# A graph layer's output product made with nodes on the PSUM partitions, the residual put in by identity products

## The chip, the core and the metric

One core of one Trainium2 chip runs the whole kernel. The metric is the device time of one execution in microseconds (us); for the kernel before it is the median of three runs. A measurement of this kernel can tell a difference of about 0.5% (3.3 us) from none.

## What is computed

Two graph layers over N = 3125 nodes with 128 features and 53125 edges, each with a residual and a layer norm over the features:

```python
x = _layernorm(x + L0(x, src, dst, edge_type_32, edge_weight1, weight, w_comp, bias))     # called x1 below
x = _layernorm(x + L1(x, edge_attr_128, src, dst, eps, W1, b1, gamma, beta, W2, b2))

def L1(node_feat, edge_feat, src, dst, eps, W1, b1, gamma, beta, W2, b2):
    msg = node_feat[src] + edge_feat
    neigh = jax.ops.segment_sum(msg, dst, num_segments=node_feat.shape[0])
    h = ((1.0 + eps[0]) * node_feat + neigh) @ W1 + b1           # N x 256
    h = (h - mean(h, axis=0)) * rsqrt(var(h, axis=0) + 1e-05) * gamma + beta
    return jax.nn.relu(h) @ W2 + b2                              # N x 128
```

The batch norm needs the mean and the variance over all nodes of every one of the 256 units, so nothing of the output layer can start before the last node's h is there. What the change touches is all behind that point: relu, the product with W2, the residual with x1, the second layer norm, the stores.

## The kernel before, in words

The first 619 us make L0, x1 and the neighbour sums of L1: a long unrolled loop over edge tiles in `narrow_sums` (TensorE, VectorE and ScalarE each have one), with gathers on GpSimd's queue, then a last series of block products on TensorE (L1041) whose results VectorE adds into the sums (L1439, two adds for a block). The order there is written out: `FINALS` lists the blocks, first those called `FILLS`, then 13 more; each product goes to one of six PSUM banks (`FINAL_BANKS`), and TensorE waits for a bank's add of six blocks ago. A flag chooses between this "narrow" way and a "wide" one for other inputs; the runs here take the narrow one.

Everything is kept **transposed**, features on the 128 partitions and nodes on the free axis: `sums[:, B, :]` holds the input of W1, `x1_t` holds x1, and `hidden` (two planes of 3125 columns, float32) holds h. The nodes are cut in seven chunks: k = 0 to 5 with 512 nodes, which is one PSUM bank of float32, and k = 6 with the 53 left over (`REST`). A chunk has four tiles of 128 nodes.

The last stage, from about 619 us on, has these steps:

- TensorE `into_hidden` (L1176): W1 stationary, 512 nodes moving, two products for a chunk, into banks 0, 1 (even chunks) or 2, 3 (odd). ScalarE `keep_hidden` (L880) adds b1 and copies to `hidden`. VectorE `hidden_stats` (L1609) takes batch-norm statistics.
- The batch norm: VectorE aggregates (L1615), ScalarE takes a square root (L885), VectorE makes scale and shift (L1617 to L1620) and signals `bn_ready`.
- The output layer, a pipeline over the chunks with two slots s = k % 2. ScalarE `relu_hidden` (L891) writes relu(scale h + shift) to `relu_stage`, two instructions for a chunk. TensorE `into_out` (L1188) multiplies it with W2 stationary into bank s, out again transposed. VectorE `second_residual` (L1625) adds b2 and x1 and writes `layer_stage` in SBUF. TensorE `turn_out` (L1139, in `turn_chunk`) transposes it tile by tile into bank 2 + s, now with nodes on the partitions. VectorE `second_stats` takes mean and variance over the features (L1557, L1560, in `statistics`), ScalarE the square root (L861), VectorE `second_shift` reciprocal and shift (L1640, L1642), and ScalarE `normalise_out` (L897) writes the normalised tiles to `out_stage`. SP's queue stores a chunk (L675) when its tiles are there.

`chunk_pipeline` writes the order on each engine: for a step it calls the stages at their lags, in the given order, first two steps unrolled, then a loop over pairs, then the rest. On ScalarE the order of a step is relu of chunk k, normalise of k - 3, square root of k - 2; on VectorE shift of k - 2, statistics of k - 1, residual of k; on TensorE product of k, transposes of k - 1. `relu_hidden` of chunk k waits for `out_mm` of chunk k - 2, since the relu buffers are two. Every engine takes its instructions in order. A float32 product appears in the trace as two weight loads and two matmuls.

`normalise` (L1562) exists for the first layer norm of the wide way; the same arithmetic in the narrow way is `chunk_norm` (L1400): VectorE subtracts the mean and multiplies by the reciprocal deviation, both [P, 1] operands.

## Time and profile before, and how to read it

| what | us |
|---|---|
| median of three runs (lowest, highest) | 666.05 (664.55, 668.14) |
| the profiled execution's own time | 670.06 |
| its span, first to last instruction | 668.2 |
| TensorE busy in the span | 545.4 (82%) |
| VectorE | 488.7 (73%) |
| GpSimd (gathers) | 414.0 (62%) |
| ScalarE | 303.5 (45%) |
| mean granted TensorE clock, share of full | 0.872 |

PE is the matmul side of TensorE and PEld its weight loads; DVE is VectorE, ACT ScalarE, SPq the DMA queue of SyncE. In the views, times are us from the start of the span unless marked ns; "L1188" is line 1188 of the kernel; an instruction's form is partitions x elements of output and input. PEclk is the granted clock as a share of 2.4 GHz, 0.50 being 1.2 GHz. A timeline row is start, duration, engine, line, operation, tiles, shape and count; several instructions that follow each other are one row, and a row's duration runs from the first one's start to the last one's end. A single instruction's own duration is longer than the step to the next one, since they overlap.

### The profile page before, as it was taken

Reading aid. Unit: us, or ns where it says so; the run is one execution under the profiler, and the core shown is the slowest. Engines: PE = TensorE matmul, PEld = TensorE weight load, DVE = VectorE, ACT = ScalarE, POOL = GpSimd, SP = SyncE. Lnnn points to the kernel's source line nnn. Section 1 sums busy time; section 2 is a strip of 40 time slices with the busy share of each in tenths; the row PEclk is TensorE's granted clock in tenths of the full one; section 3 lists DMA queues with packets and bytes.
Section 4 is the critical chain, followed back from the end, with each engine's and each line's share of the span. In section 5 each row is a group of like instructions: output and inputs, shape, how many; then the busy total and the mean of one; then the engine's idle time right before and its main releaser. Section 6 shows DMA issues by size and latency. Waiting matters only on the chain.

```text
span 668.2 us, 13132 instructions
## 1 busy us (share of the span) xinstructions
PE 545.4 (82%) x3874; PEld 439.0 (66%) x3874; DVE 488.7 (73%) x1852; ACT 303.5 (45%) x689; POOL 414.0 (62%) x434
## 2 busy tenths in 40 slices
PE   4779777877798868888797889598986999999774
PEld 3569676567685757766786758586765887767231
DVE  6998988679976678884798856988648883541535
ACT  9736545464442544533544435344434452100656
POOL 6777777777777777777777777777777740000000
PEclk9978769787787869897789879798979899999977
DMA  5424667555756366584566656757747469700003
GB/s 129 117 53 126 190 182 192 170 136 166 222 158 205 112 175 204 163 248 138 171 184 194 213 164 199 216 165 245 236 107 241 123 183 366 281 1 2 0 10 89
DMA packets 96220, 108.21 MB, mean 162 GB/s; under 512 B 10757, under 2 KB 80630, under 8 KB 96146
## 3 DMA queue, kind: packets, MB, share of 16 engines
q1 hardware_dynamic: 80082, 79.25, 38.0%
q0 software_dynamic: 13312, 27.29, 15.2%
q10 hardware_dynamic: 2752, 0.79, 0.6%
q8 instruction: 33, 0.54, 0.4%
q14 instruction: 41, 0.34, 0.2%
HBM read 81.73 MB, written 25.56 MB: 161 GB/s over the span
## 4 chain that ended last, share of the span: by engine, by line
PE 38%; DVE 25%; POOL 13%; issue 9%; DMA 5%; ACT 5%; DVEq 3%; SPq 1%; ACTq 0%
POOL gathered_flat L707 13%; PE psum L1041 12%; PE psum L1016 7%; PE psum L986 7%; DVE etype_hot L1370 5%; PE psum L992 4%; DVE sums_flat L1479 4%; PE psum L1007 4%; DVE etype_hot L1367 3%; DVE weighted L1291 3%; DVE adj_flat L1455 2%; DVE adj_flat L1267 2%; DMA gathered_flat<-in_x_dram,src_i 2%; DMA adjacency<-adj_flat 2%; PE psum L1176 1%
## 5 line engine op out<-in xcount | busy, mean ns | idle before, releaser
L707 POOL DMA_INDIRECT gathered_flat<-in_x_dram,src_i x416 | 411.7, 990 | 129.1 <-issue 123.1
L986 PE MATMUL psum<-weighted,gathered_flat 128*128 128x160 f32 (+1 forms) x832 | 162.7, 326 | 38.4 <-DMA gathered_flat<-in_x_dram,src_i 16.3
L986 PEld LDWEIGHTS psum<-weighted,gathered_flat 128*128 128x128 f32 x832 | 145.6, 224 | 54.8 <-issue 34.6
L794 ACT ACTIVATE gathered_flat<-psum 128x25 f16<-128x25 f32 x182 | 35.0, 192 | 238.2 <-PE psum L1007 231.6
L1370 DVE TENSOR_SCALAR etype_hot<-iota_key,key_t 128x300 f16<-128x300 f16 (+1 forms) x416 | 134.1, 324 | 0.0
L1479 DVE TENSOR_TENSOR sums_flat<-psum,sums_flat 128x180 f32 x208 | 71.6, 344 | 84.3 <-PE psum L992 56.2
L770 ACT ACTIVATE adj_flat<-zero_col 128x450 f16<-128x450 f32 x208 | 107.9, 574 | 42.3 <-DMA adjacency<-adj_flat 31.9
L992 PEld LDWEIGHTS psum<-hot,attrs 128*128 128x128 f32 x832 | 126.2, 217 | 0.0
L992 PE MATMUL psum<-hot,attrs 128*128 128x20 f32 (+1 forms) x832 | 121.7, 263 | 0.0
L1007 PE MATMUL psum<-etype_hot 128*128 128x300 f16 (+2 forms) x624 | 108.7, 286 | 0.0
L796 ACT ACTIVATE adj_flat<-psum 128x475 f32 x182 | 107.3, 590 | 0.2 <-issue 0.2
L1367 DVE TENSOR_SCALAR etype_hot<-iota_key,gathered_flat 128x128 f16<-128x128 f16 x416 | 104.9, 252 | 0.2
L1041 PE MATMUL psum<-sums_flat 128*128 128x288 f16 (+1 forms) x546 | 76.6, 297 | 3.3 <-DVE sums_flat L1439 3.2
L1007 PEld LDWEIGHTS psum<-etype_hot 128*128 128x128 f16 x624 | 68.5, 133 | 8.9
L1291 DVE TENSOR_TENSOR weighted<-hot,coef 128x640 f32<-128x640 f32 x104 | 72.7, 739 | 1.8
L1041 PEld LDWEIGHTS psum<-sums_flat 128*128 128x128 bf16 (+1 forms) x546 | 54.0, 101 | 23.3 <-issue 8.9
L1455 DVE TENSOR_TENSOR adj_flat<-gathered_flat,adj_flat 128x25 f16 x182 | 47.9, 263 | 21.0 <-DVE adj_flat L1455 14.8
L1439 DVE TENSOR_TENSOR sums_flat<-psum,sums_flat 128x144 f32 x124 | 37.7, 304 | 33.3 <-PE psum L1041 17.6
L1016 PE MATMUL psum<-sums_flat,gathered_flat 128*128 128x512 f32 (+1 forms) x112 | 53.7, 617 | 4.3 <-DVE sums_flat L1439 4.3
L1041 PE MATMUL psum<-coef,sums_flat 128*128 128x288 f16 x294 | 45.1, 309 | 9.9 <-DVE sums_flat L1439 9.8
L1041 PEld LDWEIGHTS psum<-coef,sums_flat 128*128 128x128 bf16 x294 | 29.9, 105 | 21.8 <-issue 13.2
L1016 PEld LDWEIGHTS psum<-sums_flat,gathered_flat 128*128 128x128 f32 x112 | 20.6, 211 | 20.2 <-issue 20.1
(143 smaller groups left out, 356.4 us busy)
## 6 DMA issues: line engine op xcount, KB each, us to landing
attrs<-in_edge_attr_dram SPq DMA_DIRECT2D x51, 512.0 KB
adjacency<-adj_flat SPq DMA_DIRECT2D x26, 900.0 KB, 4.9
gathered_flat<-in_x_dram,src_i POOLq DMA_INDIRECT x416
sums_flat<-adjacency SPq DMA_DIRECT2D x11, 576.0 KB, 6.5
coef<-adjacency SPq DMA_DIRECT2D x20, 288.0 KB, 6.7
sums_flat<-adjacency SPq DMA_DIRECT2D x6, 648.0 KB, 7.6
sums_flat<-adjacency SPq DMA_DIRECT2D x10, 288.0 KB, 6.4
etype_hot<-adjacency SPq DMA_DIRECT2D x1, 1656.0 KB, 10.3
```

The lines of the kernel that those rows point to most:

```text
L707: pool.indirect_dma_start(gathered[:, t % (RING * GROUP), :], None, x[:, :], bass.IndirectOffsetOnAxis(src_i[:, t:t + 1], 0)).then_inc(gat ...
L770: piece = nc.scalar.activation(adj_ring[:, s, j * size:(j + 1) * size], zero_col[:, 0:1].to_broadcast([P, size]), ACT.Copy)
L796: nc.scalar.activation(target[:, :, bass.ds(places[u % GU] + 1, WIN - 1)], counts[:, :, 1:WIN], ACT.Copy).then_inc(counts_copied, 1)
L986: nc.tensor.matmul(ps[:, 0:B, STARTS[i]:STARTS[i] + WIDTHS[i]], gathered[:, (u * UNIT + i) % (RING * GROUP), 0:F], weighted_tiles(s, i)[:, ...
L992: last = nc.tensor.matmul(ps[:, B, STARTS[i]:STARTS[i] + WIDTHS[i]], attrs[:, s * GROUP + j, :], hot_tiles(s, i)[:, u % GU, :], start=(i = ...
L1007: last = nc.tensor.matmul(adj_counts(u)[:, :, lo:hi], low_hot[:, u % KEYRING, i, :], source[:, :, lo - STARTS[i]:hi - STARTS[i]], start=(i ...
L1016: product = nc.tensor.matmul(bank, w_base[:, b, :], sums[:, b, k * CHUNK:k * CHUNK + n], start=(b == 0), stop=(b == B - 1))
L1041: product = nc.tensor.matmul(psum[:, bank, 0:BLOCK * SPREAD], x1_part(k, c)[0:rows, i * F:(i + 1) * F], counts[0:rows, :, :], start=(h == ...
L1291: last = nc.vector.tensor_tensor(weighted_tiles(s % 2, i), hot_tiles(s % 2, i).unsqueeze(2).to_broadcast([P, HALF, B, n]), coef[:, g * GRO ...
L1367: nc.vector.tensor_scalar(low_hot[:, u % KEYRING, i, :], iota_key[:, 0:P], low_t[:, t:t + 1], None, ALU.is_equal)
L1370: last = nc.vector.tensor_scalar(key_hot[:, u % KEYRING, i, 0:n], iota_key[:, 0:n], key_t[:, t:t + 1], None, ALU.is_equal)
L1479: nc.vector.tensor_tensor(window, unit_psum(u), window, ALU.add).then_inc(added, 1)
```

## The change

Relu is written in place in `hidden`. The output is made with nodes on the partitions: a relu tile (128 units x 128 nodes) is stationary and W2's half (128 x 128) moves, so a tile's output needs no transpose. Each chunk has a PSUM bank of its own (`OUT_BANKS`, seven of the eight). Before them, x1 with b2 added is put in the same banks by products of x1's tiles (stationary) with the identity (moving), with `start` on a bank's first tile and no `stop`, so that the W2 products accumulate on it; TensorE has these behind `into_hidden` in its queue, with a wait for the banks that `keep_hidden` still reads. b2 is added to x1 beforehand, in place, by one VectorE instruction over 128 x 3125 (`bias_x1`), put behind the third of the last 13 block adds. `second_residual`, `turn_out`, `second_shift` and `normalise_out` are gone; VectorE normalises with `normalise` (reciprocal, then one tensor_scalar for a tile out of PSUM with two [P, 1] operands). Its order is statistics of k, normalise of k - 1. ScalarE's is relu of k, square root of k - 2. The pipeline's loops are unrolled.

```diff
@@ -143,6 +143,8 @@
+    ALL_CHUNKS = tuple((k, CHUNK) for k in range(CHUNKS)) + ((CHUNKS, REST),)
+    OUT_BANKS = (4, 5, 6, 7, 2, 3, 0)
@@ -328,7 +330,6 @@
-        relu_stage = sums[:, 2:4, 0:2 * CHUNK].rearrange("p s (j n) -> p s j n", j=2)
@@ -670,12 +668,13 @@
-            def store_out(k, s, n):
-                wait_alone(sp, out_ready, (k + 2) * CT + len(tiles_of(n)))
-                sp.dma_start(rows_of(out, k, n), out_stage[:, bass.ds(k * CT, CT), :] if n == CHUNK
+            def store_out(k, n):
+                sp.wait_ge(out_ready, k * CT + len(tiles_of(n)))
+                sp.dma_start(rows_of(out, k, n), out_stage[:, k * CT:(k + 1) * CT, :] if n == CHUNK
...
-            chunk_pipeline(sp, store_out)
+            for k, n in ALL_CHUNKS:
+                store_out(k, n)
@@ -885,28 +883,23 @@
-            def relu_hidden(k, s, n):
-                act.wait_ge(out_mm, k + 1)
+            def relu_hidden(k, n):
...
-                    nc.scalar.activation(relu_stage[:, s, j, 0:n], hidden[:, j, span(k, n)], ACT.Relu,
-                                         bias=bn_shift[:, j:j + 1], scale=bn_scale[:, j:j + 1]).then_inc(relu_ready, 1)
-            def normalise_out(k, s, n):
-                act.wait_ge(shift_ready, k + 1)
-                for i, rows in tiles_of(n):
-                    nc.scalar.activation(out_stage[0:rows, bass.ds(k * CT + i, 1), :].rearrange("p t f -> p (t f)"),
-                                         psum[0:rows, 2 + s, i * P:(i + 1) * P], ACT.Identity,
-                                         bias=ln_shift[0:rows, s, i:i + 1],
-                                         scale=ln_rstd[0:rows, s, i:i + 1]).then_inc(out_ready, 1)
-            chunk_pipeline(act, relu_hidden, None, deviations(1), normalise_out, order=(0, 3, 2))
+                    units = hidden[:, j, k * CHUNK:k * CHUNK + n]
+                    nc.scalar.activation(units, units, ACT.Relu, bias=bn_shift[:, j:j + 1],
+                                         scale=bn_scale[:, j:j + 1]).then_inc(relu_ready, 1)
+            for k, n in ALL_CHUNKS:
+                relu_hidden(k, n)
+                if k >= 2:
+                    deviations(1)(k - 2, k % 2, CHUNK)
+            for k, n in LATE_CHUNKS:
+                deviations(1)(k, k % 2, n)
...
-            pe.sem_inc(out_mm, 2)
-            pe.sem_inc(out_turned, 2)
@@ -1179,22 +1172,30 @@
-            pe.wait_ge(bn_ready, 1)
-            def into_out(k, s, n):
-                pe.wait_ge(relu_ready, k * 2 + 2)
-                pe.wait_ge(out_t_ready, k + 1)
+            def x1_into_out(k, n):
+                if OUT_BANKS[k] < 4:
+                    pe.wait_ge(hidden_ready, 18 if OUT_BANKS[k] < 2 else 16)
+                for i, rows in tiles_of(n):
+                    first = k * CHUNK + i * P
+                    nc.tensor.matmul(psum[0:rows, OUT_BANKS[k], i * P:(i + 1) * P], x1_t[:, first:first + rows],
+                                     ident[:, :], start=(i == 0), stop=False)
+            pe.wait_ge(x1_biased, 1)
+            for k, n in ALL_CHUNKS:
+                x1_into_out(k, n)
+            def into_out(k, n):
...
-                    last = nc.tensor.matmul(psum[:, s, 0:n], w2_sb[:, j, :], relu_stage[:, s, j, 0:n],
-                                            start=(j == 0), stop=(j == 1))
+                    pe.wait_ge(relu_ready, 2 * k + j + 1)
+                    for i, rows in tiles_of(n):
+                        first = k * CHUNK + i * P
+                        last = nc.tensor.matmul(psum[0:rows, OUT_BANKS[k], i * P:(i + 1) * P],
+                                                hidden[:, j, first:first + rows], w2_sb[:, j, :],
+                                                start=False, stop=(j == 1 and (i + 1) * P >= n))
...
-            def turn_out(k, s, n):
-                pe.wait_ge(out_t_ready, k + 3)
-                pe.wait_ge(out_ready, k * CT + CT)
-                turn_chunk(2 + s, layer_stage[:, s, :], n).then_inc(out_turned, 1)
-            chunk_pipeline(pe, into_out, turn_out)
+            for k, n in ALL_CHUNKS:
+                into_out(k, n)
@@ -1524,7 +1524,13 @@
+                    if n == len(FILLS) + 2:
+                        bias_x1()
...
+            def bias_x1():
+                nc.vector.tensor_scalar(x1_t[:, :], x1_t[:, :], b2_col[:, 0:1], None, ALU.add).then_inc(x1_biased, 1)
@@ -1601,6 +1607,7 @@
+                bias_x1()
@@ -1619,30 +1626,22 @@
-            def second_residual(k, s, n):
-                dve.wait_ge(out_mm, k + 3)
-                dve.wait_ge(out_turned, k + 1)
-                nc.vector.scalar_tensor_tensor(layer_stage[:, s, 0:n], psum[:, s, 0:n], b2_col[:, 0:1],
-                                               x1_t[:, span(k, n)], ALU.add, ALU.add).then_inc(out_t_ready, 1)
-            def out_tile(s, i, rows):
-                return psum[0:rows, 2 + s, i * P:(i + 1) * P]
-            def second_stats(k, s, n):
-                dve.wait_ge(out_turned, k + 3)
-                statistics(1, k, s, n, lambda i, rows: out_tile(s, i, rows))
-            def second_shift(k, s, n):
-                c, top = len(tiles_of(n)), min(n, P)
-                dve.wait_ge(ln_std_ready[1], k + 1)
-                dve.wait_ge(out_ready, k * CT + CT)
-                nc.vector.reciprocal(ln_rstd[0:top, s, 0:c], ln_std[0:top, s, 0:c]).then_inc(ln_rstd_ready[1], 1)
-                dve.wait_ge(ln_rstd_ready[1], k + 1)
-                nc.vector.scalar_tensor_tensor(ln_shift[0:top, s, 0:c], ln_mv[0:top, s, 0:c, 0], -1.0,
-                                               ln_rstd[0:top, s, 0:c], ALU.mult, ALU.mult).then_inc(shift_ready, 1)
-            chunk_pipeline(dve, second_residual, second_stats, second_shift, order=(2, 1, 0))
+            def out_tile(k, i, rows):
+                return psum[0:rows, OUT_BANKS[k], i * P:(i + 1) * P]
+            def second_stats(k, n):
+                dve.wait_ge(out_mm, k + 1)
+                statistics(1, k, k % 2, n, lambda i, rows: out_tile(k, i, rows))
+            def second_norm(k, n):
+                normalise(1, k, k % 2, n, lambda i, rows: out_tile(k, i, rows),
+                          lambda i, rows: out_stage[0:rows, k * CT + i, :], out_ready)
+            for k, n in ALL_CHUNKS:
+                second_stats(k, n)
+                if k:
+                    second_norm(k - 1, CHUNK)
+            second_norm(CHUNKS, REST)
```

## Rows read from the trace of the kernel before

**Rows 1.** The page, chain that ended last: its share by engine.
```profile
PE 38%; DVE 25%; POOL 13%; issue 9%; DMA 5%; ACT 5%; DVEq 3%; SPq 1%; ACTq 0%
```

**Rows 2.** Busy time, clock and DMA in stretches of the last stage.
```profile
core 0: us, PE busy (x) PEld busy (x) DVE busy (x) ACT busy (x) POOL busy (x), PEclk, DMA share, GB/s
619.00:632.20 13.20, 11.27 (x28) 4.75 (x28) 6.12 (x11) 7.83 (x12) 0.00 (x0) 1.00 0.00 1
632.20:634.20 2.00, 0.00 (x0) 0.00 (x0) 1.57 (x4) 1.98 (x5) 0.00 (x0) 0.98 0.00 0
634.20:636.60 2.40, 0.00 (x0) 0.00 (x0) 1.83 (x9) 0.97 (x3) 0.00 (x0) 0.50 0.00 0
...
638.20:644.20 6.00, 6.00 (x7) 2.44 (x8) 0.75 (x1) 2.81 (x4) 0.00 (x0) 0.50 0.00 0
644.20:665.10 20.90, 12.93 (x47) 5.98 (x45) 13.73 (x70) 15.63 (x40) 0.00 (x0) 0.91 0.23 64
```

**Rows 3.** The chain in order of time, first products to the first statistics.
```profile
638.18 6.75 PE psum L1188 x8
644.93 0.45 PE psum L1139 x4
645.40 0.90 DVE ln_part L1557 x4
```

**Rows 4.** Timeline of VectorE, a chunk in the steady part.
```profile
654.34 0.89 DVE L1557 BATCH_NORM_STATS2 ln_part<-psum 128x6 f32<-128x128 f32 x4 [0.56 <-PE psum L1139]
655.38 0.38 DVE L1560 BATCH_NORM_AGGREGATE ln_mv<-ln_part 128x2 f32<-128x6 f32 x4 [0.15 <-DVE ln_part L1557]
655.78 0.75 DVE L1625 SCALAR_TENSOR_TENSOR attrs<-psum,b_col,sums_flat 128x512 f32<-128x512 f32 x1
656.45 0.17 DVE L1640 RECIPROCAL ln_rstd<-ln_std 128x4 f32<-128x4 f32 x1
...
657.35 0.89 DVE L1557 BATCH_NORM_STATS2 ln_part<-psum 128x6 f32<-128x128 f32 x4 [0.54 <-PE psum L1139]
```

**Rows 5.** Timeline of TensorE and ScalarE around the batch norm.
```profile
624.53 7.60 PE L1176 MATMUL psum<-sums_flat,gathered_flat 128*128 x20 [1.08 <-ACT sums_flat L880]
...
636.57 2.93 ACT L891 ACTIVATE sums_flat<-sums_flat,bn_shift,bn_scale 128x512 f32<-128x512 f32 x4 [0.82 <-DVE bn_shift L1620]
```

**Rows 6.** Timeline, end of the kernel: the last ScalarE tile and the last stores.
```profile
664.36 1.29 SPq L675 DMA_DIRECT2D out_dram<-gathered_flat  x2
...
664.56 0.45 ACT L897 ACTIVATE gathered_flat<-psum,ln_shift,ln_rstd 53x128 f32<-53x128 f32 x1 [0.41 <-DVE ln_shift L1642]
```

**Rows 7.** Timeline of TensorE at full clock, 545 to 562 us.
```profile
556.82 0.65 PE L986 MATMUL psum<-weighted,gathered_flat 128*128 128x160 f32 x4
557.30 0.52 PE L992 MATMUL psum<-hot,attrs 128*128 128x20 f32 x4
```

**Rows 8.** Timeline of TensorE at the low clock, 42 to 54 us.
```profile
48.46 1.19 PE L986 MATMUL psum<-weighted,gathered_flat 128*128 128x160 f32 x4
```

**Rows 9.** VectorE instructions by form, busy us and mean ns of one.
```profile
L1400 DVE TENSOR_SCALAR sums_flat<-sums_flat,ln_mv,ln_rstd 128x128 f32<-128x128 f32 x4 | 1.1, 342 | 0.0
L1410 DVE TENSOR_SCALAR sums_flat<-sums_flat 128x512 bf16<-128x512 f32 x1 | 0.4, 427 | 0.0
L1412 DVE TENSOR_TENSOR sums_flat<-sums_flat 128x512 f32<-128x512 f32 x1 | 0.7, 693 | 0.0
L1383 DVE TENSOR_TENSOR sums_flat<-psum,attrs 128x512 f32<-128x512 f32 x1 | 0.7, 692 | 6.3 <-PE psum L1024 6.3
L1267 DVE TENSOR_SCALAR adj_flat<-psum,relation_col 128x512 bf16<-128x512 f32 x26 | 18.1, 730 | 0.3 <-PE psum L923 0.3
```

**Rows 10.** Timeline of VectorE, normalising a chunk of the first layer norm.
```profile
574.57 1.12 DVE L1400 TENSOR_SCALAR sums_flat<-sums_flat,ln_mv,ln_rstd 128x128 f32<-128x128 f32 x4
```

**Rows 11.** Timeline of VectorE, block adds before the last stage.
```profile
609.46 0.76 DVE L1439 TENSOR_TENSOR sums_flat<-psum,sums_flat 128x144 f32 x2 [1.29 <-PE psum L1041]
...
618.85 0.76 DVE L1439 TENSOR_TENSOR sums_flat<-psum,sums_flat 128x144 f32 x2 [8.64 <-PE psum L1041]
```

More of the change, by code:

```diff
@@ L342, in gnn_resnorm_kernel @@
         ln_rstd = sb("ln_rstd", [P, 2, CT])
-        ln_shift = sb("ln_shift", [P, 2, CT])
         psum = ctx.enter_context(nc.psum_tensor("psum", [P, 8, 512], F32))
@@ L458, in gnn_resnorm_kernel @@
         out_mm = sem("out_mm")
-        out_t_ready = sem("out_t_ready")
-        out_turned = sem("out_turned")
-        shift_ready = sem("shift_ready")
+        x1_biased = sem("x1_biased")
         out_ready = sem("out_ready")
@@ L735, in _ @@
             act.sem_inc(agg_relu, 2)
-            act.sem_inc(out_ready, 2 * CT)
             act.sem_inc(x1_t_ready, 2)
@@ L1214, in _ @@
             dve.sem_inc(res_ready[0], 2)
-            dve.sem_inc(out_t_ready, 2)
             dve.wait_ge(const_ready, 2)
```

## The prediction, made before the changed kernel was run

> **What bounds the kernel now.** I read the page's chain first. It gives 38% of the span to TensorE and 25% to VectorE [rows 1], but that is an average over a long front part that the change leaves alone, so the reader should go on to the stretches of the last stage [rows 2]. Four things are to be seen there. TensorE ends `into_hidden` at 624.53 + 7.60 = 632.1 us [rows 5] and then has nothing to do while VectorE and ScalarE make the batch norm. Its clock falls from full to 0.50 (1.2 GHz) in that idle time, at about 634.2, and is still 0.50 from 638.2 to 644.2 although PE is busy without a gap [rows 2]. In the chain, the first eight output matmuls therefore take 6.75 us, then come the transposes, and VectorE's first statistics start at 645.40 [rows 3], 8.8 us behind the scale and shift (ready at 636.57, when the first relu starts [rows 5]). From then on the work goes by chunks: statistics start at 654.34 and again at 657.35, a period of 3.01 us, in which VectorE waits 0.54 us for transposes [rows 4]. The last tile is normalised at 664.56 + 0.45 = 665.0 and the last store lands at 668.2, a tail of 3.2 us [rows 6].
>
> So there are two places for a gain: the 8.8 us before the first statistics, and the period.
>
> **The start.** The change puts 25 identity products (six chunks of four tiles, one of one) into the batch norm's time. Each is a float32 product of 128 columns, two weight loads and two matmuls. The nearest rows are the products of 160 and 120 columns at full clock: four matmuls with their loads go from 556.82 to 557.30, so 0.12 us for one [rows 7]. The row's 0.65 is three such steps and the last one's own latency, 0.29. With 20 columns the four take 0.52 [rows 7]; less a latency of 0.25, a little shorter, that is 0.09 a step, which is the weight load alone. So at 140 columns the load is mostly hidden behind the matmul before. I take 0.24 us for a product; bounds 0.19 (load alone) and 0.43 (load and matmul one after the other, 2 x (0.09 + 0.12)). 25 x 0.24 = 6.0 us, from 632.1 to 638.1. The relu of chunk 0 is ready at 636.57 + 2 x 0.73 = 638.0 (four relus take 2.93 [rows 5]). So the identity products fit the gap almost exactly; what of them is past 638.0 costs 0.1 us. The banks of chunks 4 to 6 wait for `keep_hidden`, long done when TensorE comes to them.
>
> Chunk 0 then needs 8 W2 products instead of four wide matmuls: 8 x 0.24 = 1.9 us, done at 640.1, statistics at 640.2. Before, 645.4. That is 5.2 us earlier, of which some 3.4 are the clock (6.75 us at half clock for two chunks, 3.4 at full) and the rest the missing residual add and transposes. It rests on the clock staying full, since TensorE no longer idles; rows 2 show it full from 619 to 632 at 85% busy.
>
> **The period.** VectorE loses the residual add (0.75 [rows 4]), the shift and the 0.54 us of waiting. It keeps statistics, 0.89 + 0.15 + 0.38 = 1.42, with its wait 1.47, and gains the normalising: reciprocal 0.17 [rows 4], 0.04 for its semaphore, and four tensor_scalars out of PSUM with two [P, 1] operands. The same instruction from SBUF takes 1.12 us for four, 0.26 from start to start [rows 9, 10]. From PSUM there is one nearby row: 128x512 takes 730 ns against 427 from SBUF, 303 more for 512 elements [rows 9]. Tensor_tensor shows no such difference (692 from PSUM, 693 from SBUF [rows 9]), so it is likely a rate by element and a quarter of it, 0.076, at 128. Bounds 0.26 (none) and 0.56 (all 303 ns at any width); I take 0.30, nearer to the quarter. Normalising a chunk is then 0.21 + 1.20 = 1.41, and VectorE's period 1.47 + 1.41 = 2.88 against 3.01: nearly nothing is gained there.
>
> The Trainium skill ("VectorE: DVE Perf Modes", Why PSUM operands drop a tier) says an SBUF float32 tensor_scalar runs at two elements a cycle and one from PSUM at one. By that rule, the trace agrees: the tensor_scalar from SBUF is faster than the tensor_tensor, the one from PSUM is not. Its table of costs (section on the TRN2 errata) has a larger fixed cost from PSUM besides, 120 cycles for 58; by it a tile would take some 0.13 us more than from SBUF, 0.39, and the end would come 2 us later than I forecast. The equal tensor_tensor rows speak against that.
>
> ScalarE's relus (1.47 a chunk) and square roots stay under 2.88, and TensorE's 1.92 too; each chunk has its own bank, so TensorE waits for relus only. The square root of chunk k - 2 sits ahead of the relu of chunk k + 1 in ScalarE's queue and waits there for the statistics; that relu is then needed one period later, by a TensorE that is ahead. It costs nothing while VectorE is the slowest.
>
> **The sum.** Chunk 1's products end at 640.1 + 1.9, its statistics start at 642.1. From there VectorE has no wait: statistics of 1, 1.47; six normalisations, 8.46; statistics of 2 to 5, 5.88; the short chunk's statistics and normalisation, one tile each, an estimate of 0.6 and 0.55. Together 17.0, so 659.1. Before 665.0: 5.9 us earlier. The tail: the two last stores now follow 0.55 us apart in place of 1.0, and SP's queue needs 1.29 us to issue two [rows 6], so up to 0.4 us is given back; I take 0.3. Net 5.6 us.
>
> **bias_x1.** One instruction of 3125 elements; at 427 ns for 512 it is 2.6 us, at 693 it is 4.2 [rows 9]. It sits between block adds, where VectorE idles 1.29 us before each add and 8.64 before the last, 618.85 [rows 11]. The three or four adds behind it come late and catch up; TensorE waits only for the add of six blocks ago, some 12 us. Cost nothing; without that cover, 2.6 to 4.2. The unrolled loops and the dropped semaphores: nothing that a row shows.
>
> The profiled execution took 670.06 us with a span of 668.2; the change would make that 662.6 and 664.5. It is 4.0 us over the median of 666.05, from which I subtract the same 5.6: **660.4**.
>
> **Rivals.**
>
> - **VectorE dearer** (the normalising binds). At 0.39 a tile the end is 2.2 us later: saving 3.4, 662.6. At the far bound, 0.56, a period of 3.9 us: six times 1.04 more, end 665.3, no gain, 666.6. For it: no row has this instruction from PSUM. Against: the tensor_tensor pair. Chance 0.14, half of it past the 0.5% line.
> - **The clock falls all the same.** If identity products do not keep it up, it falls at 634.2 as before [rows 2]. The 16 products left then take twice as long (the four matmuls of 0.65 us take 1.19 at the low clock [rows 7, 8]), which delays all by some 4 us; the clock returns after some 6 us of work. End 663 to 665, saving 0 to 2: 664 to 666. Chance 0.12.
> - **TensorE becomes the bound, and the kernel slower.** One mechanism: the weight load of every 128 columns is not hidden, or the clock stays low through the stage. A product costs 0.43 to 0.48, the identity products end at 643 to 644, a chunk takes 3.4 to 3.8 us, more than VectorE. End 669 to 672: 4 to 7 us slower, 670 to 673. It decides from 0.37 us for a product: there the gain is nil. For it: 50 more weight loads than needed before, and no row with 128-column moving operands of this kind. Against: the rows of 160 and 120 columns. Chance 0.08.
> - **It doesn't do what it says:** the W2 products start late for another reason, such as ScalarE's queue (a relu behind a square root) or the stores crowding at the end. Saving 1 to 3: 663 to 665. Chance 0.08.
>
> **How the numbers follow.** The forecast has 0.58: 658.5 to 662 with the bounds of a product (0.19 makes it 1.5 earlier) and of a tile (0.26 and 0.335: 1 us either way). The range goes to the first two rivals, 658.3 to 665.0, and leaves out 2 in 10. Faster by over 0.5% (3.3 us; the resolution of a measurement here): 0.58 + 0.07 + a little of the last = 0.67. Slower: 0.08. Same: 0.25.
>
> **What would show it.** The clock in stretches after 632: 1.00 up to 650. TensorE busy without a gap from 632.1, the last identity product near 638. First statistics at 640.2. Four tensor_scalars out of PSUM in 1.3 us or less, VectorE without idle time from the statistics of chunk 1 on. Block adds at the same times from the sixth behind bias_x1 on. The last tile at 659, the tail 3.5. A first statistics start past 644 would make the clock or the product's price wrong; a period over 3.1 the tile's.

## The result, and the profile after

| | before | changed |
|---|---|---|
| median of eight runs each on one chip, us | 667.21 | 661.44 |
| lowest, highest | 664.55, 669.91 | 659.68, 664.44 |
| ratio, with its 95% interval | | 0.9917 (0.989 to 0.9944) |
| profiled execution, its span | 670.06, 668.2 | 664.44, 662.6 |
| mean granted TensorE clock | 0.872 | 0.889 |

The changed kernel is 5.5 us faster at the ratio (667.2 x 0.0083), with an interval of 3.7 to 7.3 us; the spans differ by 5.6. That is past the 0.5% that a measurement here resolves, but not by much. The stretches of the last stage of the changed kernel (columns as in [rows 2]):

```profile
613.80:627.00 13.20, 11.06 (x55) 6.22 (x53) 2.96 (x6) 3.83 (x6) 0.00 (x0) 1.00 0.01 2
...
633.00:639.00 6.00, 6.00 (x53) 5.70 (x53) 2.84 (x11) 4.55 (x9) 0.00 (x0) 1.00 0.00 0
...
639.00:650.00 11.00, 10.64 (x94) 10.13 (x92) 8.76 (x46) 8.22 (x16) 0.00 (x0) 1.00 0.17 49
```

Where [rows 2] had TensorE without work and a clock that fell to 0.50 at 634.2 and stayed there to 644.2, it is now busy for all of 633 to 639 and the clock reads 1.00 up to 650. The timeline from there:

```profile
624.77 7.61 PE L1169 MATMUL psum<-sums_flat,gathered_flat 128*128 x20 [1.07 <-ACT sums_flat L878]
...
632.21 5.94 PE L1180 MATMUL psum<-ident,sums_flat 128*128 128x128 f32 x50
...
636.82 4.34 ACT L889 ACTIVATE sums_flat<-sums_flat,bn_shift,bn_scale 128x512 f32<-128x512 f32 x6 [0.82 <-DVE bn_shift L1627]
...
638.08 11.23 PE L1192 MATMUL psum<-gathered_flat,sums_flat 128*128 128x128 f32 x96
640.17 0.89 DVE L1563 BATCH_NORM_STATS2 ln_part<-psum 128x6 f32<-128x128 f32 x4 [3.39 <-PE psum L1192]
...
641.96 0.89 DVE L1563 BATCH_NORM_STATS2 ln_part<-psum 128x6 f32<-128x128 f32 x4 [0.36 <-PE psum L1192]
```

The fifty matmuls of the identity products (x1 into the banks) follow the last product of W1 and end where the W2 products begin, 638.1. The first layer-norm statistics start at 640.17; in [rows 3] it was 645.40. From the second statistics on, VectorE waits for no other engine. A chunk in the steady part, against [rows 4], and the one place where VectorE stops:

```profile
644.76 0.88 DVE L1563 BATCH_NORM_STATS2 ln_part<-psum 128x6 f32<-128x128 f32 x4
...
645.79 0.38 DVE L1566 BATCH_NORM_AGGREGATE ln_mv<-ln_part 128x2 f32<-128x6 f32 x4
646.09 0.15 DVE L1571 RECIPROCAL ln_rstd<-ln_std 128x4 f32<-128x4 f32 x1
...
646.27 1.37 DVE L1574 TENSOR_SCALAR gathered_flat<-psum,ln_mv,ln_rstd 128x128 f32<-128x128 f32 x4
...
647.55 0.89 DVE L1563 BATCH_NORM_STATS2 ln_part<-psum 128x6 f32<-128x128 f32 x4
...
650.35 0.88 DVE L1563 BATCH_NORM_STATS2 ln_part<-psum 128x6 f32<-128x128 f32 x4
651.76 0.38 DVE L1566 BATCH_NORM_AGGREGATE ln_mv<-ln_part 128x2 f32<-128x6 f32 x4 [0.53 <-DVE ln_part L1563]
```

The period is 647.55 - 644.76 = 2.79 us, 3.01 before. The statistics of chunk k + 1 stand between those of k and the normalising of k, so the square root on ScalarE is covered. In chunk 4 the aggregates start 1.41 us behind their statistics (651.76 - 650.35), where chunk 2 has 1.03 (645.79 - 644.76): a stop of 0.38 us, with VectorE's own statistics as the only thing waited for. It recurs at the same place in changed_again, x1_late, no_x1 and bias_last, whose VectorE order there is the same. What it is the traces do not say.

The end, against [rows 6], and the waits of the stage:

```profile
658.47 0.40 DVE L1574 TENSOR_SCALAR gathered_flat<-psum,ln_mv,ln_rstd 53x128 f32<-53x128 f32 x1
```

```profile
ACT ln_std L859 <- DVE ln_mv L1566: 9.1, 6, 2.5
...
DVE ln_part L1563 <- PE psum L1192: 3.8, 2, 3.4
```

VectorE waits for TensorE twice in the stage (3.8 us, 3.4 of it before the first statistics) where before it waited in every whole chunk. ScalarE waits 9.1 us for VectorE: it has room, which the experiments below use. And `bias_x1`, with the block adds behind it, against [rows 11]:

```profile
594.46 1.84 DVE L1533 TENSOR_SCALAR sums_flat<-sums_flat,b_col 128x3125 f32<-128x3125 f32 x1
...
596.21 0.75 DVE L1439 TENSOR_TENSOR sums_flat<-psum,sums_flat 128x144 f32 x2
...
601.52 0.76 DVE L1439 TENSOR_TENSOR sums_flat<-psum,sums_flat 128x144 f32 x2 [0.93 <-PE psum L1034]
```

The block behind `bias_x1` is added 1.2 us late, and the next ones follow 1.2 us apart. The fifth (601.52) is on time: it waits 0.93 us for TensorE, and in the kernel before, 0.25 us ahead all along here, it starts at 601.27. The sixth has the full wait of 1.29 again.

### The profile page after: what moved, and what is told of

It is laid out like the page before. It is cut to its first block, busy times and chain, and to the rows that moved or that the text cites. A ratio compares the mean times of both kernels' runs of the same rounds, so it can differ in the third digit from the quotient of the medians.

```text
span 662.6 us, 13215 instructions
## 1 busy us (share of the span) xinstructions
PE 539.0 (81%) x3971; PEld 441.8 (67%) x3971; DVE 492.0 (74%) x1864; ACT 296.2 (45%) x664; POOL 418.0 (63%) x434
## 4 chain that ended last, share of the span: by engine, by line
PE 35%; POOL 24%; DVE 20%; issue 11%; DMA 7%; ACT 2%; DVEq 1%; SPq 0%; ACTq 0%
POOL gathered_flat L706 24%; PE psum L1034 13%; PE psum L979 6%; DMA gathered_flat<-in_x_dram,src_i 5%; PE psum L1009 5%; PE psum L985 4%; DVE etype_hot L1370 3%; PE psum L1000 3%; DVE sums_flat L1479 2%; DVE adj_flat L1267 2%; DVE etype_hot L1367 2%; DVE weighted L1291 2%; PE psum L1169 1%; DVE gathered_flat L1574 1%; DMA attrs<-in_edge_attr_dram 1%
## 5 line engine op out<-in xcount | busy, mean ns | idle before, releaser
L979 PE MATMUL psum<-weighted,gathered_flat 128*128 128x160 f32 (+1 forms) x832 | 160.1, 321 | 49.8 <-DMA gathered_flat<-in_x_dram,src_i 27.1
L979 PEld LDWEIGHTS psum<-weighted,gathered_flat 128*128 128x128 f32 x832 | 141.9, 219 | 67.6 <-issue 33.1
L985 PEld LDWEIGHTS psum<-hot,attrs 128*128 128x128 f32 x832 | 124.5, 215 | 0.0
L1367 DVE TENSOR_SCALAR etype_hot<-iota_key,gathered_flat 128x128 f16<-128x128 f16 x416 | 106.9, 257 | 0.1
L1009 PE MATMUL psum<-sums_flat,gathered_flat 128*128 128x512 f32 (+1 forms) x112 | 51.5, 596 | 4.3 <-DVE sums_flat L1439 4.3
```

Source lines behind the costliest of these rows:

```text
L979: nc.tensor.matmul(ps[:, 0:B, STARTS[i]:STARTS[i] + WIDTHS[i]], gathered[:, (u * UNIT + i) % (RING * GROUP), 0:F], weighted_tiles(s, i)[:, ...
L985: last = nc.tensor.matmul(ps[:, B, STARTS[i]:STARTS[i] + WIDTHS[i]], attrs[:, s * GROUP + j, :], hot_tiles(s, i)[:, u % GU, :], start=(i = ...
L1009: product = nc.tensor.matmul(bank, w_base[:, b, :], sums[:, b, k * CHUNK:k * CHUNK + n], start=(b == 0), stop=(b == B - 1))
L1367: nc.vector.tensor_scalar(low_hot[:, u % KEYRING, i, :], iota_key[:, 0:P], low_t[:, t:t + 1], None, ALU.is_equal)
```

## The experiments

On the chips of the experiments the whole kernel took some 800 us (before: medians of 799.5 to 813.2), since the part ahead of the last stage took 130 to 140 us longer there; why was not studied. The last stage is the same in its rows (the twenty W1 matmuls take 7.60 to 7.61 us in every run), so stages are compared, in us from the start of the first relu, and ratios are against the kernel before on the same chip. Each row is one profiled execution. The end of a span is read to 0.1 us, so in the last two columns a difference under 0.1 says nothing:

| kernel | first statistics | from first to second | first statistics to end of last tile | from there to end of span | relu to end of span |
|---|---|---|---|---|---|
| before | 8.83 | 2.89 | 19.61 | 3.19 | 31.63 |
| changed | 3.35 | 1.79 | 18.70 | 3.73 | 25.78 |
| changed_again | 3.37 | 1.78 | 18.67 | 3.76 | 25.80 |
| tile_price | 8.74 | 2.89 | 20.14 | 3.20 | 32.08 |
| old_warm | 5.76 | 2.89 | 20.04 | 3.20 | 29.00 |
| x1_late | 11.01 | 1.79 | 18.71 | 3.75 | 33.47 |
| no_x1 | 4.75 | 2.69 | 19.59 | 3.82 | 28.16 |
| bias_last | 3.35 | 1.79 | 18.70 | 3.78 | 25.83 |
| split34 | 3.35 | 1.79 | 16.32 | 4.03 | 23.70 |
| split34_again | 3.36 | 1.78 | 16.30 | 4.05 | 23.71 |
| split135 | 3.36 | 1.79 | 16.39 | 4.34 | 24.09 |
| best | 2.95 | 1.79 | 16.31 | 4.03 | 23.29 |
| halved_store | 2.95 | 1.79 | 16.31 | 4.12 | 23.38 |

The first question is the start: of the 5.48 us by which the first statistics come earlier, how much is the clock, and how much the way from products to statistics?

**old_warm**, the kernel before with the identity products in the idle time, into banks that nobody reads:

```diff
             chunk_pipeline(pe, into_hidden)
+            for i in range(25):
+                nc.tensor.matmul(psum[:, 4 + i // 4 % 4, i % 4 * P:(i % 4 + 1) * P], x1_t[:, i * P:(i + 1) * P] if i < 24 else x1_t[:, 0:P],
+                                 ident[:, :], start=True, stop=True)
             pe.wait_ge(bn_ready, 1)
```

> The kernel before, with 25 identity products of x1's tiles put on TensorE between into_hidden and its wait for bn_ready, into banks 4 to 7 that nothing reads: they only keep TensorE busy. Theory (the clock is the larger part of the early start): the granted clock stays 1.00 from 632 on, the first eight L1188 matmuls take 3.5 us in place of 6.75, the first statistics start 5.5 us behind the first relu in place of 8.8, the chunk period stays 3.0, and the kernel is 3.3 us faster than before (0.995). Rival (nodes on the rows is the gain, the clock is not): less than 1 us from the kernel before.

Timeline of TensorE, then the stretches (columns as above):

```profile
760.90 5.81 PE L1183 MATMUL psum<-ident,sums_flat 128*128 128x128 f32 x50
...
767.11 3.67 PE L1191 MATMUL psum<-sums_flat,gathered_flat 128*128 128x512 f32 x8 [0.41 <-issue]
...
785.45 1.08 PE L1139 MATMUL psum<-ident,attrs 128*128 128x128 f32 x4 [1.89 <-DVE attrs L1628]
```

```profile
766.00:780.00 14.00, 12.28 (x43) 5.71 (x41) 7.46 (x34) 11.22 (x23) 0.00 (x0) 1.00 0.08 22
...
783.00:786.00 3.00, 1.11 (x9) 0.99 (x8) 2.27 (x11) 1.80 (x6) 0.00 (x0) 0.92 0.46 133
786.00:791.30 5.30, 0.99 (x4) 0.30 (x2) 2.51 (x15) 3.64 (x11) 0.00 (x0) 0.50 0.27 76
```

The eight W2 matmuls of [rows 3] take 3.67 us in place of 6.75: 3.08, and the first statistics come 3.07 earlier. That is the clock alone, with nothing else of the change. (tile_price, further down, is the kernel before without these fillers on such a chip: its eight take 6.65.) The stage is 2.63 shorter, not 3.07: the clock falls at about 785.5 (0.92 over the 3 us to 786), where the transposes of the last whole chunk run, and 0.43 is given back between first statistics and last tile. Those transposes take 1.08 us for four; in the timeline of the kernel before it is 0.66:

```profile
659.59 0.66 PE L1139 MATMUL psum<-ident,attrs 128*128 128x128 f32 x4 [1.88 <-DVE attrs L1625]
```
The ratio is 0.9979 (0.9951 to 1.0007), too small for the runs to tell from none. The other 2.41 us (5.76 - 3.35) belong to the shorter way: in old_warm the residual add starts at 769.11, the transposes start when TensorE is through with chunk 1's matmuls (770.62), and the statistics start at 771.26, 2.15 behind the add. Now they start when chunk 0's products are done. Of the 2.41, 2.15 is that way, and 0.35 is that the first product starts 1.26 us behind the first relu (638.08 - 636.82) in place of 1.61 (767.11 - 765.50), since it needs the relu of one half of the units and not of both (then it is the identity products that it waits for, see best); chunk 0's products and the way to VectorE are 0.09 longer.

**x1_late**, the changed kernel with the identity products behind the batch norm:

```diff
             pe.wait_ge(x1_biased, 1)
+            pe.wait_ge(bn_ready, 1)
             for k, n in ALL_CHUNKS:
                 x1_into_out(k, n)
```

> The changed kernel with TensorE's wait for bn_ready put ahead of the identity products, so that they no longer lie beside the batch norm. Theory: TensorE idles 4.5 us, its clock falls to 0.50, the 25 products start at 636.8 and take about 9 us (half of them at half clock), the first statistics come 7 to 8 us later than in the changed kernel, the kernel is 7 us slower than it and 1 to 2 us slower than the kernel before. Rival (only the 5.9 us of the products themselves count, the clock stays up): 4.5 us slower than the changed kernel, still 1 us faster than before.

```profile
767.94 8.88 PE L1180 MATMUL psum<-ident,sums_flat 128*128 128x128 f32 x50 [4.55 <-DVE bn_shift L1628]
```

```profile
765.30:767.80 2.50, 0.00 (x0) 0.00 (x0) 1.99 (x9) 1.10 (x2) 0.00 (x0) 0.89 0.00 0
767.80:771.00 3.20, 3.06 (x14) 3.09 (x15) 0.00 (x0) 3.17 (x5) 0.00 (x0) 0.50 0.02 5
```

The stage takes 33.47 us, 7.69 more than the changed kernel's and 1.84 more than before; the ratio to before is 1.0042 (1.0012 to 1.0072). It is in the first statistics (7.66): the W2 products start 8.92 behind the first relu (776.75 - 767.83) in place of 1.26, since the identity products are no longer covered and take 8.88 us for 5.94, the clock having fallen. So here the change pays only with its identity products in the batch norm's time.

**no_x1**, the changed kernel without the identity products: x1 and b2 are left out of the result.

```diff
             pe.wait_ge(x1_biased, 1)
-            for k, n in ALL_CHUNKS:
-                x1_into_out(k, n)
+            pe.wait_ge(hidden_ready, 18)
...
-                                                start=False, stop=(j == 1 and (i + 1) * P >= n))
+                                                start=(j == 0 and i == 0), stop=(j == 1 and (i + 1) * P >= n))
```

> The changed kernel without the identity products: the second residual with x1 and b2 is left out, the rest is the same. Theory: although TensorE has 5.9 us less to do, its clock falls in the idle time, chunk 0's products take 3.8 us in place of 1.9 and chunk 1's nearly so, the first statistics come 1.5 to 2 us later and the kernel is 1.5 to 2.5 us slower than the changed one (3.5 us faster than before). Rival (the identity products cost what they take, hidden or not): equal to the changed kernel or up to 1 us faster.

```profile
766.40 13.84 PE L1191 MATMUL psum<-gathered_flat,sums_flat 128*128 128x128 f32 x96 [5.39 <-ACT sums_flat L889]
...
770.19 0.89 DVE L1562 BATCH_NORM_STATS2 ln_part<-psum 128x6 f32<-128x128 f32 x4 [4.78 <-PE psum L1191]
```

```profile
769.00:772.00 3.00, 3.00 (x16) 3.00 (x16) 1.27 (x8) 1.12 (x4) 0.00 (x0) 0.51 0.00 0
772.00:775.00 3.00, 3.00 (x29) 3.00 (x28) 1.93 (x11) 2.02 (x4) 0.00 (x0) 1.00 0.00 0
```

Less work, and a longer stage: 28.16 us against 25.78. Without the identity products TensorE idles 5.39 us, its clock is 0.50 to 772, sixteen matmuls fit in 3 us where at full clock 29 do, the first statistics come 1.40 later and the second 0.90 later still. So the identity products bring more than they would save if the residual cost nothing: they are what keeps the clock up. The ratio to before is 0.9974 (0.9947 to 1.0002).

**tile_price**, the kernel before with ten more tensor_scalars on VectorE ahead of the pipeline, to measure the disputed price by itself:

```diff
+            at = 0
+            for width, times in ((P, 3), (CHUNK, 2)):
+                for source in (psum[:, 6, 0:width], x1_t[:, 0:width]):
+                    for i in range(times):
+                        nc.vector.tensor_scalar(sums[:, 5, at:at + width], source, bn_ms[:, 0:1], bn_rstd[:, 0:1],
+                                                ALU.subtract, ALU.mult)
+                        at += width
```

> The kernel before with ten instructions added on VectorE while it waits for the first W2 products: the normalising tensor_scalar with two [P, 1] operands, three times 128 columns and twice 512, each from PSUM and from SBUF. Theory (the surcharge from PSUM goes by the element): start to start 0.34 us from PSUM and 0.26 from SBUF at 128 columns; at 512, 0.3 us apart. Rival (a fixed surcharge): the same difference at both widths. The kernel's end does not move, since they lie in VectorE's idle time.

The instructions of that line (duration ns as least/median/most; the least ones are 128 wide, the most 512), and their timeline:

```profile
L1625 DVE TENSOR_SCALAR sums_flat<-psum,bn_ms,bn_rstd x5: 402/406/803, 767.5 to 769.9; 128x128 f32<-128x128 f32 x3, 128x512 f32<-128x512 f32 x2
L1625 DVE TENSOR_SCALAR sums_flat<-sums_flat,bn_ms,bn_rstd x5: 337/341/539, 768.5 to 771.1; 128x128 f32<-128x128 f32 x3, 128x512 f32<-128x512 f32 x2
```

```profile
767.50 1.04 DVE L1625 TENSOR_SCALAR sums_flat<-psum,bn_ms,bn_rstd 128x128 f32<-128x128 f32 x3
768.46 0.85 DVE L1625 TENSOR_SCALAR sums_flat<-sums_flat,bn_ms,bn_rstd 128x128 f32<-128x128 f32 x3
```

PSUM as the source costs 406 - 341 = 65 ns more at 128 elements and 803 - 539 = 264 at 512: 0.51 and 0.52 ns an element, with no fixed part. From start to start a tile is 0.32 us from PSUM ((1.04 - 0.406) / 2) and 0.257 from SBUF.

The end was not to move, and it did: the stage is 32.08 us for 31.63. VectorE stops once here too, 0.39 us with nothing waited for that the profile shows, at a place where the kernel before has no such stop:

```profile
784.11 0.75 DVE L1632 SCALAR_TENSOR_TENSOR attrs<-psum,b_col,sums_flat 128x512 f32<-128x512 f32 x1 [0.39 <-issue]
```

**bias_last**, `bias_x1` behind the last block add, where VectorE has no idle time before it:

```diff
-                    if n == len(FILLS) + 2:
-                        bias_x1()
                 dve.wait_ge(nbr_added, BLOCK * (NRUNS + len(FINALS)))
+                bias_x1()
```

> The changed kernel with bias_x1 moved behind the last block add, ahead of the signal that starts into_hidden, where nothing covers it. Theory (the placement among the block adds costs nothing since VectorE idles there): from the last block add to the first W1 matmul there are 1.8 us more, the price of the one instruction (1.84 us in the changed kernel's trace). Rival (the last adds were held up by it in the changed kernel too): less than 1 us more.

```profile
756.65 1.85 DVE L1532 TENSOR_SCALAR sums_flat<-sums_flat,b_col 128x3125 f32<-128x3125 f32 x1
756.78 3.67 PE L1169 MATMUL psum<-sums_flat,gathered_flat 128*128 128x512 f32 x8 [1.07 <-issue]
...
761.41 2.47 DVE L1615 BATCH_NORM_STATS2 bn_part<-sums_flat 128x6 f32<-128x512 f32 x4 [2.91 <-ACT sums_flat L878]
```

A miss: no cost, 1.07 us before the first W1 matmul as in the changed kernel (1.06). The W1 products start 0.13 us after `bias_x1` does, so the signal to TensorE, which is an increment by VectorE's queue and not bound to this instruction, didn't wait for its end; and VectorE then waits 2.91 us for h anyway. What `bias_x1` costs where nothing covers it was not tried.

The next question is what bounds the stage now. If it is VectorE, work given to ScalarE, which waits 9.1 us, shortens it. Two tiles of every chunk for each engine (split_norm) would let both read one bank with nothing to order them, and have no measured time; so ScalarE gets whole chunks.

**split34**: ScalarE normalises chunks 3 and 4, by which time its relus are done. The core of the edit (VectorE makes scale and shift for a chunk, as `second_shift` did, and SP waits for both engines' tiles):

```diff
+    ACT_TILES = (0, 0, 0, 4, 4, 0, 0)
...
+            def normalise_out(k):
+                if ACT_TILES[k]:
+                    act.wait_ge(shift_ready, k + 1)
+                for i in range(CT - ACT_TILES[k], CT):
+                    nc.scalar.activation(out_stage[:, k * CT + i, :], psum[:, OUT_BANKS[k], i * P:(i + 1) * P], ACT.Identity,
+                                         bias=ln_shift[:, k % 2, i:i + 1],
+                                         scale=ln_rstd[:, k % 2, i:i + 1]).then_inc(out_act, 1)
...
-                normalise(1, k, k % 2, n, lambda i, rows: out_tile(k, i, rows),
-                          lambda i, rows: out_stage[0:rows, k * CT + i, :], out_ready)
+                nc.vector.scalar_tensor_tensor(ln_shift[0:top, s, 0:c], ln_mv[0:top, s, 0:c, 0], -1.0,
+                                               ln_rstd[0:top, s, 0:c], ALU.mult, ALU.mult).then_inc(shift_ready, 1)
+                for i, rows in tiles_of(n)[:c - ACT_TILES[k]]:
```

> The changed kernel with ScalarE normalising the whole of chunks 3 and 4 (VectorE makes reciprocal and shift for every chunk and normalises the others). Theory (VectorE's order alone sets the period): the two chunks lose 1.37 us each and every chunk gains 0.2 for the shift, so the last tile comes 1.4 us earlier: the first relu to the end of the span 24.4 us in place of 25.8, ratio to the kernel before about 0.99 of a kernel of 665 us. Rival (ScalarE's in-order queue passes the wait on): no earlier end, or a later one.

```profile
783.14 0.88 DVE L1583 BATCH_NORM_STATS2 ln_part<-psum 128x6 f32<-128x128 f32 x4
...
784.73 0.88 DVE L1583 BATCH_NORM_STATS2 ln_part<-psum 128x6 f32<-128x128 f32 x4
784.84 1.51 ACT L907 ACTIVATE gathered_flat<-psum,ln_shift,ln_rstd 128x128 f32<-128x128 f32 x4
```

The stage is 23.70 us, 2.08 less than the changed kernel's. VectorE's statistics of chunk 5 follow those of chunk 4 after 1.59 us (784.73 - 783.14), in the changed kernel after 3.17, of which 0.38 is the stop. First statistics to last tile is 2.38 us shorter: eight tiles less, 2 x 1.28 = 2.56, and the stop, which is not there, 0.38, against seven instructions for the shift at 0.08 each, 0.56. The tail gives 0.3 back. The expectation had 1.4 for it all, with 0.2 for a shift and no stop. The ratio is 0.991 (0.988 to 0.994). So VectorE's order is the bound, as expected.

**split135**, the same with `ACT_TILES = (0, 4, 0, 4, 0, 4, 0)`:

```diff
-    ACT_TILES = (0, 0, 0, 4, 4, 0, 0)
+    ACT_TILES = (0, 4, 0, 4, 0, 4, 0)
```

> The same with ScalarE normalising chunks 1, 3 and 5. Theory: three chunks off VectorE, 4.1 us less and 1.3 for shifts more; ScalarE's normalise of chunk 1 stands ahead of the relu of chunk 5, which comes about 1 us later but still in time for VectorE; the first relu to the end of the span 23.0 to 23.5 us. Rival: the relu of chunk 5 becomes what VectorE waits for, and the gain is no more than that of chunks 3 and 4.

```profile
784.90 2.62 PE L1212 MATMUL psum<-gathered_flat,sums_flat 128*128 128x128 f32 x20 [1.51 <-ACT sums_flat L900]
785.38 0.88 DVE L1583 BATCH_NORM_STATS2 ln_part<-psum 128x6 f32<-128x128 f32 x4
...
786.80 0.38 DVE L1586 BATCH_NORM_AGGREGATE ln_mv<-ln_part 128x2 f32<-128x6 f32 x4 [0.53 <-DVE ln_part L1583]
...
787.35 0.88 DVE L1583 BATCH_NORM_STATS2 ln_part<-psum 128x6 f32<-128x128 f32 x4
...
790.75 0.18 DVE L1661 RECIPROCAL ln_rstd<-ln_std 128x4 f32<-128x4 f32 x1
...
791.16 1.50 ACT L907 ACTIVATE gathered_flat<-psum,ln_shift,ln_rstd 128x128 f32<-128x128 f32 x4
```

A miss: 24.09 us, 0.39 more than split34 with one chunk more on ScalarE. The relu of chunk 5 stands behind the normalising of chunk 1 in ScalarE's queue, and TensorE waits 1.51 us for it, but that costs nothing: VectorE takes chunk 5's statistics at 787.35 without a wait. Up to the reciprocal of chunk 5 both kernels have taken two chunks from VectorE, and it stands 17.84 us behind the first relu here (790.75 - 772.91) and 17.45 in split34 (786.85 - 769.40). The 0.39 between them is the stop of 0.38, which this kernel has (786.80) and split34 has not. Behind it the third chunk gains nothing: ScalarE's chunk 5 is itself the last work (791.16 + 1.50). The ratio is 0.9921 (0.9888 to 0.9953).

**changed_again and split34_again**, the two kernels unaltered, run on another chip, side by side with the next one. The rows of the table repeat within 0.03 us.

> The changed kernel itself, beside the two others of this call on the same chip, to compare them directly. From the first relu to the end of the span 25.8 us, 5.9 us less than in the kernel before; ratio to it 0.991 to 0.993.

> ScalarE normalises chunks 3 and 4, again: 23.7 us from the first relu to the end, 2.1 us faster than the changed kernel, ratio to the kernel before 0.988 to 0.990 if this chip is as fast as the first.

The ratios to the kernel before there are 0.9916 (0.9892 to 0.9939) and 0.9897 (0.9864 to 0.993).

**best**, split34 with the identity products of chunks 5 and 6 moved behind the W2 products of chunk 2, so that the first W2 products don't wait for them:

```diff
-            for k, n in ALL_CHUNKS:
+            for k, n in ALL_CHUNKS[:5]:
                 x1_into_out(k, n)
...
                 into_out(k, n)
+                if k == 2:
+                    for late in ALL_CHUNKS[5:]:
+                        x1_into_out(*late)
```

> The same, and the identity products of chunks 5 and 6 moved behind the W2 products of chunk 2. Theory (the last of the 25 identity products end 0.5 us after the first relu is ready and so set the start): 20 of them end at 4.7 us, before that relu; TensorE idles 0.6 us, too short for the clock to fall; the first W2 product and the first statistics come 0.5 us earlier, the products of chunk 3 come 1.2 us later, still in time; 23.2 us from the first relu to the end. Rival (chunk 3 comes too late for VectorE, or the start is set by the second relu): 0 to 0.2 us.

```profile
764.61 4.69 PE L1200 MATMUL psum<-ident,sums_flat 128*128 128x128 f32 x40
...
770.08 5.62 PE L1212 MATMUL psum<-gathered_flat,sums_flat 128*128 128x128 f32 x48 [0.78 <-ACT sums_flat L900]
```

The first statistics come 0.40 us earlier than in split34, and the stage is 23.29 us, 2.5 less than the changed kernel's. TensorE now waits for the relu (0.78 us), where in the changed kernel the relu's result waited for TensorE. The ratio is 0.9898 (0.9867 to 0.993). The intervals of the three kernels overlap: that this one beats the changed kernel is shown by the stage, not by the whole time.

**halved_store**, best with the store of chunk 5 as two of 128 KB:

```diff
+                if k == CHUNKS - 1:
+                    for half in range(2):
+                        sp.wait_ge(out_ready, dve_tiles_to(k) - 2 + 2 * half)
+                        sp.wait_ge(out_act, act_tiles_to(k))
+                        first = k * CT + 2 * half
+                        sp.dma_start(out[first * P:(first + 2) * P, :].rearrange("(t p) f -> p t f", p=P),
+                                     out_stage[:, first:first + 2, :]).then_inc(out_done, 16)
```

> The kernel with ScalarE on chunks 3 and 4 and the late identity products, and chunk 5's store cut in two of two tiles each, the first issued when its tiles are normalised. Theory (the end is set by chunk 5's store of 256 KB, 4.2 to 4.6 us behind its last tile, not by the small store behind it): half of it is under way 0.7 us before, the end comes 0.4 to 0.6 us earlier, 22.8 us from the first relu to the end, the tail behind the last tile 3.5 us in place of 4.0. Rival (the small last store sets the end, and SP's queue has one store more to issue): the end comes at the same time or 0.3 us later.

```profile
796.28 0.99 SPq L693 DMA_DIRECT2D out_dram<-gathered_flat  x2
...
797.39 0.27 SPq L684 DMA_DIRECT2D out_dram<-gathered_flat  x1
```

A miss: the tail is 4.12 us for 4.03, the same as far as the spans can tell, and not the 3.5 expected. With one issue more SP's queue ends its last at 797.66, 0.78 us behind the last tile (796.88). In best it ends 0.30 behind (788.77 against 788.47):

```profile
785.82 2.95 SPq L684 DMA_DIRECT2D out_dram<-gathered_flat  x4
```
The rest, from the end of the last issue to the end of the span, is 3.34 against 3.73. What is won there is lost in the queue, and the end stays where it was.

## Why the prediction was right, point by point

The forecast was 5.6 us less; measured, 5.5 by the ratio and 5.6 between the profiled spans. (660.4 was 5.6 below the three runs' 666.05; the eight have 667.21 before and 661.44 after.) The mechanism is as forecast. That the number is right to 0.1 is luck: several terms are off by 0.2 to 0.4 us, and cancel. By its steps:

- **Identity products.** 0.24 us for one: 5.94 / 25 = 0.24. They end where it said, 638.1, by two small errors: 5.94 us for 6.0, from 632.21 for 632.1. The clock was to read 1.00 up to 650; it does, and no_x1 and old_warm show that it is these products that hold it: the rival that the clock falls all the same is refuted, and so is the one with TensorE as the bound, which needed 0.37.
- **The start.** First statistics at 640.17 (640.2), second at 641.96 (642.1). Its split, 3.4 for the clock and the rest for the shorter way, measured 3.07 and 2.41. The clock's part was sized 0.3 high: the eight matmuls take 3.67 us at full clock, not half of 6.75. And 640.17 stands on a first relu that came 0.25 late; from that relu it is 3.35 us for 3.6.
- **A tile's price.** 0.30 was taken; it is 0.32. Four, from the first's start to the next group's, are 646.27 to 647.55, 1.28 for 1.20. The far bound of 0.56 and the 0.39 of the first rival are out. What the forecast took from the tensor_tensor pair holds, a surcharge by the element: 65 and 264 ns at 128 and 512 are a quarter and the whole, and 264 is near its 303. The Trainium skill ("VectorE: DVE Perf Modes", Why PSUM operands drop a tier) lets the SBUF form run at two elements a cycle and the PSUM form at one, and the trace agrees: from 128 to 512 elements the SBUF form grows by 0.52 ns an element and the PSUM form by 1.03. The Trainium skill's table of costs on that page (section on the TRN2 errata) has a larger fixed cost from PSUM too, which by the prediction's estimate would have made a tile 0.39: the measurement differs, and no fixed part is there.
- **The period.** 2.79 for 2.88. The tiles were 0.08 a chunk dearer; statistics with their wait and the reciprocal 0.17 cheaper (644.76 to 646.27, 1.51, for 1.47 + 0.21), since the reciprocal starts before the aggregates have ended and nothing of its semaphore shows. The forecast also had VectorE without idle time from chunk 1's statistics on; the stop of 0.38 us in chunk 4 makes that one period 3.17. From the second statistics to the last tile it is 16.91 us (641.96 to 658.87) for 17.0: the six normalisations some 0.3 dearer, the stop 0.4 more, the statistics with the short chunk 0.8 cheaper. So the total is right by errors of opposite sign.
- **The tail.** 0.3 was to be given back; it is 0.54 (3.73 for 3.19), and SP's queue, the forecast's reason, doesn't explain it: its last issue ends 0.30 us behind the last tile now (644.87 + 14.30 = 659.17), and ended 0.64 behind it before (664.36 + 1.29 = 665.65). The tail was measured from the short chunk's tile. From the end of chunk 5's last tile it is the same in both kernels: 657.00 + 1.36 = 658.36 to 662.6 is 4.2 us, and before 662.47 + 1.51 = 663.98 to 668.2 is 4.2 too. So between these two the end keeps its distance from chunk 5's tiles, whose store is 256 KB, and the short chunk's tile only comes 0.5 us sooner behind them. It is no constant: it is 4.2 to 4.3 in all traces but split34, split34_again, best and halved_store, which have 4.6 to 4.7. There chunk 4's last tile is done just 0.57 us before chunk 5's (split34: 787.93 and 788.50), 1.97 in the changed kernel, so the two large stores come close together. That this lengthens the tail was not tested; halved_store shows only that cutting chunk 5's store doesn't help, and what sets the 4.2 us is open. Timelines of the changed kernel and of the kernel before:

```profile
657.00 1.36 DVE L1574 TENSOR_SCALAR gathered_flat<-psum,ln_mv,ln_rstd 128x128 f32<-128x128 f32 x4
```

```profile
662.47 1.51 ACT L897 ACTIVATE gathered_flat<-psum,ln_shift,ln_rstd 128x128 f32<-128x128 f32 x4 [0.44 <-DVE ln_shift L1642]
```

- **`bias_x1`.** Its cost on the path was nothing, as forecast, but its size was wrong: 1.84 us, under the bounds of 2.6 and 4.2. A row of 512 elements (427 ns) multiplied by 6.1 multiplies its fixed part too. The cover was misread as well: at that place VectorE idles 0.45 us before an add (the adds are 1.21 us apart there) and not the 1.29 of [rows 11], which in the kernel before begins with the fourth add behind it (599.22). The adds still caught up at the fifth and TensorE's block products kept their step.
- **The front part** ended 0.25 us later in this execution (first relu at 636.82 for 636.57), with nothing in it that the change explains; it was not forecast.

The sum of the stage: 5.48 (start) + 0.91 (first statistics to last tile, 19.61 - 18.70) - 0.54 (tail) = 5.85, less the 0.25 is 5.6. The first has old_warm and no_x1 behind it; what the front's 0.25 is was not studied.

## What to carry to other kernels

Independent products put into TensorE's idle time ahead of a critical stretch can pay twice: they were free there, and the stretch started at full clock. Look in the stretches for the clock just behind a long wait (0.50 for 6 us here), and price the filler by its own time at full clock against the length of the wait. A mapping that makes the output in the layout in which it is needed was worth the steps it drops at the pipeline's start here (2.41 us) and little behind it (0.91 over seven chunks); in the steady part count the busiest engine's instructions, and give work to the engine that waits, in the order in which it comes free.

## What the runs showed that was not expected

- A stretch with less work took longer: no_x1 leaves 50 matmuls out and its stage is 2.4 us longer, through the clock alone.
- The clock also fell inside the pipeline: in old_warm at about 785.5, while TensorE waited 1.89 us for the last whole chunk's transposes, and 0.43 us of the gain went with it. In the kernel before it is still 1.00 at that chunk's transposes and falls at about 661.4.
- The clock stayed at 0.50 through several us of unbroken matmuls before it was full again: in no_x1 from 766.4 to 771.9, in x1_late from 767.9 to 774.1, in [rows 2] from 638.2 to 644.4.
- VectorE stops once for 0.38 or 0.39 us with no other engine to wait for. Where it does moves with its order of instructions: at chunk 4 in the changed kernel, at a residual add in tile_price, nowhere to be seen in split34 and best. In split135 it cost as much as the difference to split34. Its cause is open.
- Two [P, 1] operands seem to cost VectorE time: a 128x512 tensor_scalar from SBUF takes 539 ns with them and 427 without ([rows 9]). The row without them also writes bf16 and has one operation, not two, so the price of the operands by themselves is not shown.
- The increment behind a VectorE instruction that nothing waits for went out 0.13 us after that instruction's start, though it ran 1.85 us (bias_last).
- Two stores of 128 KB in place of one of 256 KB left the tail as it was.
